# Row maxima carried as a row of the queries, biases folded into weights, and the exponentials' low half split by query half

## The reference, cut to what matters

```python
# layer 0: non-local attention per image, 64 embedding channels, no biases
f = softmax(theta.T @ phi / sqrt(64));  x = x + proj_w @ (f applied to x)
# layer 1: on tokens t (4, 1024, 128), z = layernorm(t)
keys = z @ Wk + bk; queries = z @ Wq + bq; values = z @ Wv + bv
t = t + softmax(queries @ keys.T / sqrt(128)) @ values
# layer 2: top 2 of 8 experts, z = layernorm(t)
gate = z @ Wg + bg; w = softmax(top 2 of gate)
t = t + sum over the two experts e: w_e * (gelu(z @ W1[e] + b1[e]) @ W2[e] + b2[e])
```

## Time and profile before

| | us |
|---|---|
| median of 3 runs | 565.32 (560.21 to 565.96) |
| span of the profiled execution | 603.2 |
| steps -2 and -1, to the first maximum of unit 1 | 0 to 41.4 |
| unit 0's step | 41.4 to 69.3 |
| units 1, 2, 3 | 69.3 to 103.5 to 137.0 to 172.7 |
| units 4, 5, 6 | 172.7 to 212.9 to 248.2 to about 278 |
| unit 7's step | 278 to about 318 |
| unit 7's outputs, routing, first tiles | 318 to 437 |
| experts | 437 to 575 |
| mixing, transposing, storing | 575 to 603.2 |

### The profile page before, as it was taken

The page is one execution under the profiler, slowest core; times in us unless marked ns, Lnnn a source line. Parts: engine busy times, 40 slices in busy tenths (PEclk is TensorE's granted clock), DMA queues, the critical chain, the costliest instruction groups (busy, mean ns, idle before and its releaser), DMA issues.

```text
span 603.2 us, 15423 instructions
## 1 busy us (share of the span) xinstructions
PE 431.2 (71%) x4139; PEld 313.6 (52%) x4140; DVE 431.8 (72%) x1303; ACT 300.6 (50%) x689; POOL 307.6 (51%) x352
## 2 busy tenths in 40 slices
PE   5668898999999899995952051610588898989626
PEld 3333565766666567663741041400476687878512
DVE  4897898988889788888684131781277788878737
ACT  4567766668866556663541000130265566656402
POOL 2012264555466654553787737027047677767720
PEclk9899999999999899998885565855699999999965
DMA  6100400000000130000011101004312222222166
GB/s 205 29 2 0 140 1 0 3 0 3 0 1 0 30 112 0 1 0 2 10 53 54 53 28 53 1 22 114 78 40 74 71 74 83 74 76 84 45 198 238
DMA packets 33493, 30.94 MB, mean 51 GB/s; under 512 B 8327, under 2 KB 27437, under 8 KB 33453
## 3 DMA queue, kind: packets, MB, share of 16 engines
q1 hardware_dynamic: 28844, 20.92, 12.2%
q0 software_dynamic: 4608, 9.51, 4.7%
HBM read 16.69 MB, written 13.73 MB: 50 GB/s over the span
## 4 chain that ended last, share of the span: by engine, by line
PE 25%; DVE 22%; issue 21%; POOL 8%; another core or an unknown queue 8%; ACT 7%; DVEq 3%; SPq 2%; DMA 2%; ACTq 1%; POOLq 0%
PE SC L529 8%; PE PV L529 7%; PE MX L529 6%; POOL ybuf L517 5%; PE PR L529 3%; DVE mx L1179 3%; ACT E L987 2%; DVE DG L1183 2%; ACT EH L911 1%; DVE TOK L1475 1%; DVE stats L1218 1%; DVE TOK L1480 1%; DVE QK L1137 1%; DVE TOK L1214 1%
## 5 line engine op out<-in xcount | busy, mean ns | idle before, releaser
L529 PE MATMUL PV<-VH,EH 128*128 128x129 f16 x512 | 98.2, 230 | 9.2 <-DVE TOK L1214 7.5
L529 PE MATMUL PV<-VL,EH 128*128 128x128 f16 x512 | 97.8, 226 | 3.6 <-issue 3.6
L529 PE MATMUL PV<-VH,EL 128*128 128x129 f16 x512 | 98.1, 228 | 2.2 <-issue 2.2
L474 POOL TENSOR_TENSOR EL<-E,EH 128x1024 f32 (+1 forms) x32 | 68.1, 2128 | 59.6 <-ACT EH L911 59.3
L517 POOL DMA_INDIRECT ybuf<-QK,yid x80 | 88.4, 1105 | 18.2 <-issue 12.8
L910 ACT ACTIVATE E<-SC 128x512 f32<-128x512 f32 x128 | 77.1, 602 | 37.5 <-PE SC L529 37.5
L529 PE MATMUL SC<-QK 128*128 128x512 f16 x320 | 91.0, 383 | 6.3 <-ACT EH L911 5.9
L438 POOL DMA_INDIRECT zbuf<-ZZ,posi x64 | 63.5, 993 | 51.9 <-DVE posi L1104 33.6
L1179 DVE TENSOR_REDUCE mx<-MX 128x1 f32<-128x1024 f32 x64 | 77.9, 1217 | 1.5 <-PE MX L529 1.1
L911 ACT ACTIVATE EH<-SC 128x512 f32 (+1 forms) x128 | 77.8, 608 | 0.0
L529 PE MATMUL MX<-EL,EH 128*128 x640 | 59.4, 246 | 2.7 <-issue 2.7
(11 more groups left out here) (195 smaller groups left out, 963.5 us busy)
## 6 DMA issues: line engine op xcount, KB each, us to landing
EH<-zbuf SPq DMA_DIRECT2D x40, 130.0 KB
X<-in_x_dram SPq DMA_DIRECT2D x4, 512.0 KB, 5.6
zbuf<-zer SPq DMA_DIRECT2D x16, 128.0 KB, 2.8
X<-in_L_ffn_W_dram SPq DMA_DIRECT2D x1, 2048.0 KB, 9.7
EL<-ybuf SPq DMA_DIRECT2D x4, 512.0 KB, 5.6
EH<-ybuf SPq DMA_DIRECT2D x4, 512.0 KB, 8.9
out_dram<-X SPq DMA_DIRECT2D x8, 256.0 KB, 3.0
ybuf<-QK,yid POOLq DMA_INDIRECT x80
```

Source lines behind the costliest of these rows:

```text
L474: nc.gpsimd.tensor_tensor(EL[:, u % 2, ds(i * 2 + 1, 1), :], E32[:, 1:2, :], EH[:, u % 2, ds(i * 2 + 1, 1), :], ALU.subtract).then_inc(e32 ...
L529: return nc.tensor.matmul(o, w, r, start=start, stop=stop)
```

## The change

- **Maxima as a row.** The reduction writes bf16. PE multiplies the column by minus the identity over a constant c (`row`: two products of one output row, 128 columns each, into MX[0:1]), ACT copies the row into channel 0 of the queries' low half, and the keys have the constant c in channel 0: so the scores' own matmuls subtract the maximum, and the diagonals and their matmuls go. In layer 0 the keys' halves are laid out so that a group of scores is two matmuls (was three), in layer 1 three (was four). A row of pair i is made in pair i+1 (PE behind the second group of scores, ACT behind the second exponentials), the last one in the first pair of the next step.
- **Constant channel 0.** POOL presets channel 0 of the normalised rows to 128. Since a layer norm sums to zero over the channels, the weights' row 0 can be subtracted from the others and the bias put in its place (`augment` on DVE in step -1, `expert_rows` on DVE ahead of unit 3's step). The bias matmuls, the gate's bias and the Gelu's bias go; Gelu becomes one instruction of 1024 columns.
- **Merged weights.** Layer 1's scores use Wq·Wkᵀ (`gram`): queries are projected with it, and the keys are the transposed rows themselves; the keys' projection of layer 1 goes.
- **Order.** Scores, exponentials and E32 go by query half: (p, h) = (0,0), (1,0), (0,1), (1,1). POOL makes EL of the first query half and does so first in its pair; DVE makes the second, now behind its second maximum.

GpSimd's presets stand ahead of its other constants, and PE's first instruction waits for all five:

```diff
+            nc.gpsimd.memset(QK[0:CE, :, 1, :], 0.0).then_inc(preset, 1)
+            nc.gpsimd.memset(QK[0:CE, :, 3, :], 0.0).then_inc(preset, 1)
+            pool.wait_ge(preset, 2)
+            nc.gpsimd.memset(QK[0:1, :, 3, :], TOP).then_inc(preset, 1)
+            nc.gpsimd.memset(ZZ[:, :, 0:1], CST).then_inc(preset, 1)
+            nc.gpsimd.memset(ZZ[:, :, P:P + 1], 0.0).then_inc(preset, 1)
```

GpSimd's pair:

```diff
-                    pool.wait_ge(sc_free, i * 4 + (2 * T * u + 6))
-                    nc.gpsimd.tensor_tensor(EL[:, u % 2, ds(i * 2 + 1, 1), :], E32[:, 1:2, :],
-                                            EH[:, u % 2, ds(i * 2 + 1, 1), :], ALU.subtract).then_inc(e32_free[1], 1)
+                    pool.wait_ge(sc_free, i * 4 + (2 * T * u + 4))
+                    c = slice(0, HALF)
+                    nc.gpsimd.tensor_tensor(EL[:, u % 2, ds(i * 2, 2), c], E32h[0], EH[:, u % 2, ds(i * 2, 2), c],
+                                            ALU.subtract).then_inc(e32_free[0], 1)
...
                 def pair(i, before):
+                    if u is not None:
+                        e_low(i)
                     if before is not None:
                         normalise(*before)
                         split(*before)
-                    if u is not None:
-                        e_low(i)
```

TensorE:

```diff
+                def row(unit, need):
+                    pe.wait_ge(mx_free, need)
+                    for p in range(2):
+                        last = mm(MX[0:1, p * P:(p + 1) * P], mxb[:, p:p + 1], negI[:, layer(unit), :], True, True)
+                    last.then_inc(mx_full, 1)
...
-                    pe.wait_ge(diag_ready, T * u + T // 2 * (h + 1))
-                    mm(o_, onesb[:], DG[:, u % 2, 4 * h:4 * h + 4, :], False, True).then_inc(sc_full, 1)
...
                     if u is not None:
-                        scores(i, 0, 1)
+                        scores(i, 1, 0)
+                    if first and u is not None:
+                        row(u, mx_base(s) + 1)
+                    if not first and m is not None:
+                        row(m, i * 3 + n_mx)
...
-                    if v is not None and v < UNITS:
+                    if v is not None and v < B:
                         projected("keys", i)
```

ScalarE:

```diff
+                def row(unit, c, need):
+                    act.wait_ge(mx_full, need)
+                    cp(QL[0:1, unit % 3, c], MX[0:1, 0:2 * P]).then_inc(mx_free, 1)
...
-                for c in range(HC):
-                    k = slice(c * TR, (c + 1) * TR)
-                    last = nc.scalar.activation(h32[:, b % 2, k], WIDE[b % 2][:, k], ACT.Gelu,
-                                                bias=b1T[:, ds(e * HC + c, 1)], scale=1 / WS)
-                last.then_inc(h_ready, 1)
+                nc.scalar.activation(h32[:, b % 2, :], WIDE[b % 2], ACT.Gelu, scale=1 / WS).then_inc(h_ready, 1)
```

VectorE (`augment`, `expert_rows`, the reduction):

```diff
+                nc.vector.scalar_tensor_tensor(out=W32[:, 2:5, :], in0=W0b[:], scalar=nvec[:, 0:1],
+                                               in1=W32[:, 2:5, :], op0=ALU.mult, op1=ALU.add)
...
+                nc.vector.scalar_tensor_tensor(out=Xw[:, c], in0=W10b[k // 2][:, k % 2 * S:(k % 2 + 1) * S],
+                                               scalar=nvec[:, 0:1], in1=Xw[:, c], op0=ALU.mult, op1=ALU.add) \
...
+                if s == 3:
+                    dve.wait_ge(w1_in, 16 * (2 + E))
+                    for k in range(PAIRS):
+                        expert_rows(k)
...
-                    nc.vector.reduce_max(mx[:, p:p + 1], MX[:], AX.X).then_inc(mx_free, 1)
+                    nc.vector.reduce_max(mxb[:, p:p + 1], MX[:], AX.X).then_inc(mx_free, 1)
```

More of the change, by code:

```diff
@@ L41 @@
 VW = P + 1
+CST = 128.0
+TOP = 2.0 ** 15
 E = 8
@@ L272, in build @@
                 {"values": (0, 0), "queries": (1, 0), "keys": (0, 1)},
-                {"rows": (0, 0), "values": (1, 0), "queries": (0, 1), "keys": (1, 1)},
+                {"rows": (0, 0), "values": (1, 0), "queries": (0, 1)},
                 {"rows": (0, 0), "logits": (1, 0)}]
@@ L925, in pair @@
                         high_x()
-                    if v is not None and v >= B:
+                    late = first and s == UNITS - 1
+                    if v is not None and v >= B and not late:
                         transposed(i)
                     if u is not None:
-                        exponentials(i, 0, 1)
+                        exponentials(i, 1, 0)
+                    if first and u is not None:
+                        row(u, slice(S - 2 * P, S), mx_base(s) + 1)
+                    if late:
+                        transposed(i)
+                    if not first and m is not None:
+                        row(m, ds(i * 256 - 256, 256), i * 3 + n_mx)
                     if first and v is not None and v < B:
@@ L1126, in _ @@
                 u, a, m, v = roles(s)
-                n_mx = mx_base(s) + (1 if v is not None and v < B else 0)
+                n_mx = mx_pairs(s)
                 if v is not None and v < B:
@@ L1311, in pair @@
                         statistics(i, 0)
+                        sums(i, 1)
                         counted(i, 0)
-                    if on_m:
-                        diagonals(i, 0)
+                    if on_v and v < UNITS:
+                        queries(i)
                     elif on_a:
```

300 lines of the change are left out of this document (164 added, 136 removed).

## The result

The changed kernel took 617.11 us (616.5 to 617.53, 4 runs) against 562.77 for the kernel before (558.85 to 565.96): ratio 1.097 [1.091, 1.102]. Forecast were 588, range 545 to 603: the side was right, but the rise is 54 us where 23 were forecast, and the time lies outside the range.

The account below looks back on a forecast made before the run. TensorE looked like the bound, with VectorE's work close beside it. 13.5 + 5.6 + 5.0 + 4.6 - 2 - 2 = +24.7, less 2 for overlap, about +23: 588 us for the median of 565.3, range 545 to 603.

Parts of the forecast that it names:

- the term for SP's queue: Ten W1 loads issued for one, row broadcasts some 60 us ahead, nothing waiting behind them in SP's queue: 0.
- the steps -1 to 1: First attention steps: pairs of step -1 +3.6 less 0.6, step 0 +2.0, step 1 +1.1.
- The pairs, +13.5: Attention pairs of units 0 to 6, four per step, mostly lengthened by new waits, unit 4 shortened: +13.5 us in all.
- the exclusion: GpSimd's low half (2.13 us) and certain VectorE instructions block each other, so VectorE's mean copy waits until R+3.3 in every pair.
- expert_rows, +4.6: Four VectorE operations of 1024 columns ahead of unit 3's step, 1.21 each, TensorE's values behind: +4.6 (0 to 6).
- The front, +5.6: TensorE's first instruction waits for GpSimd's presets, 10.8 instead of 4.30; first product from 9.33 to about 14.9: +5.6.
- nothing either way: ScalarE gains a row copy per pair (0.28) and loses or splits a key copy: no net cost.
- Step -1 and the borders: Step -1: `augment` +2.0, pairs +3.6 less 0.6, +5.0 together; 2 taken off the whole for overlap at step borders.
- Experts and unit 7's step, -4: One Gelu for four in the experts, -2; GpSimd's low half moved into its idle gap in unit 7's step, -2.
- Rival 1: The exclusion costs nothing, the mean copy slipping ahead of GpSimd's low half; pairs 7.7 to 7.9, 558 us; chance 0.27.
- rival 2: The engines' work decides, waits fall into slack; pairs 7.0 to 7.2 us, 537 us; chance 0.14.
- rival 3: Only the front costs; pairs as long as now, +15 less 4 left, 576 us; chance 0.14.

Follow-up runs that it names:

- e2: e1 with GpSimd's old order restored, normalise and split ahead of its low half: 659.7 us, kernel before beside it 607.8; stretch from first to last maximum 277.0.
- e6: e1 with VectorE's mean copy and variance addition each made by a sum over one element: 656.3 us, kernel before beside it 604.3; stretch 275.6.
- e1: Changed kernel with W1 loaded whole on 128 partitions and b1 laid over row 0 afterwards: 659.3 us, kernel before beside it 607.8; stretch 284.1.
- e3: Kernel before with its W1 load cut into partition 0, then partitions 1 to 127: 622.6 us against 607.8, 1.032 [1.020, 1.043].
- e14: Kernel before with its W1 load cut into partitions 0 to 126, then partition 127: 584.2 us against 564.8, one run.
- e9: e5 with the expert rows spread in eight instructions over steps 2 and 3, ScalarE's wait moved to its W1 scaling: 584.3 us, 1.037 [1.033, 1.041].
- e15: e10 with Wq, Wk, Wv and Wg loaded whole and biases laid over row 0: 581.2 us against 564.8, 1.027 [1.022, 1.033].
- e5: e2 with ScalarE's row copy ahead of tile 1's exponentials and VectorE's keys ahead of its low half at early step borders: 657.0 us against 604.3.
- e0: The changed kernel unedited, run again: 618.0 us against 564.2 for the kernel before, 1.098 [1.093, 1.103].
- e10: e9 with fills on VectorE and TensorE waiting for presets and constants only ahead of step -1: 582.8 us against 564.2, 1.026 [1.022, 1.030].
- e11: Kernel before with GpSimd's subtraction for W1's low half spread over steps 4 and 5: 559.7 us against 564.2, 0.992 [0.990, 0.995].

## Where the prediction failed, and where it held

The step that failed is the term for SP's queue, put at 0: it was worth some 16 us. Next come the steps -1 to 1, forecast 6.1 us longer and 17.7 longer in the trace. Point by point, the forecast against the traces:

- **The pairs, +13.5: the sum right, by two errors.** Steps 0 to 6 without the one long pair are 14.6 longer, but steps 2 to 6 only 3.8 (10.4 forecast) and steps 0 and 1 10.8 (3.1). Single pairs took 9.3 to 9.6 in step 2 (9.1 forecast), 9.6 to 9.7 in step 5 (9.3), 9.0 in step 1 (8.7), 9.0 to 9.3 in step 4 (9.3), 8.7 to 9.0 in step 3 (9.3), 8.2 to 8.5 in step 6 (8.9); and step 4's last pair fell from 11.64 to 9.15, which I had not looked at. The mechanism is shown: e2 and e6 take the exclusion away in two ways and get 7.1 and 8.5 us back. Two of its details were off: it strikes the mean copy in steps 1, 2, 4 and 5 (up to 2.13 us) and the square in steps 3 and 6 (up to 1.78), in all 14 of 32 copies and 22 of 32 squares over 0.3 us (4 and 1 before), not the copy in every pair; and with it gone the pairs return to the length before, not below.
- **SP's queue, "nothing waits in SP's queue behind them: 0": the step that failed.** The load of 127 partitions ran on one DMA engine and SP stood 74.66 us with the copies of row 0 behind it. I counted ten issues and did not price the one whose form had changed. Worth 15.7 us in the trace, 16.2 in e1; the form alone, in the kernel before, cost 19.2 (e3) and 18.0 (e14).
- **expert_rows, +4.6: the size right (4.9), its place not.** ScalarE's wait for the rows stands ahead of its exponentials of step 3; with that the rows cost 7.9 (the pair is 16.8 in e1, 8.9 in the kernel before) or 8.2 (8.6 in e9). I had put what is queued behind VectorE's instructions, not what is queued behind ScalarE's wait for them.
- **The front, +5.6: right to 0.2** (fills 2.65 against 2.6, first instruction 11.22 against 10.8, first product 15.06 against 14.9). To the first maximum I had 2.0 more, it was 4.0 more: 1.4 between the first product and the last key copy, where the keys' copy in two parts (0.77 instead of 0.38, in 4 pairs) was left at "nothing either way", and 2.5 from the low half of x to the maximum, where `augment` stands. e15 gets 6.1 of the 9.7 back.
- **Step -1 and the borders: too small.** Without the 2.0, step -1 was forecast +3.0 and is +6.9, step 0 +2.0 and is +5.8, step 1 +1.1 and is +5.0. The last pairs of these steps are 2.3 to 3.5 longer each, where I took 2 off "for what overlaps at the step borders". No clock was in the forecast, and part of this is the clock. Two pairs of step -1 (6.15, 4.9 forecast) ran at a granted clock of 0.50, the lower level of 1.2 GHz; the third took 5.32 at 0.82. Ahead of them TensorE had stood 3.63 us for the augmented weights (the two rows below). A pair of step 0 took 7.07 at 0.83, and 6.76 at 1.00 in e5 and e9 with their other edits; in the earlier trace rows it is 6.43 at 1.00. So some 1.7 us of step -1 and 1 us of step 0 are the clock, an estimate from these pairs; the border pairs, at 0.69 to 0.85, are not separated.

```profile
27.95 0.47 PE L586 MATMUL PV<-ident,W 128*128 128x128 f32 x1 [3.63 <-DVE W L1114]
...
41.80:47.10 5.30, 3.23 (x21) 1.93 (x20) 3.73 (x5) 1.90 (x5) 0.00 (x0) 0.82 0.00 0
```

- **Experts and unit 7's step, -4:** the Gelus, first to last, take 118.4 to 120.8 us in the changed kernel, e0, e9, e10 and e15 against 123.0 to 126.0 in e11 to e14, -2 to -8 for -2; unit 7's gain was not seen apart. The whole second half is 285 against 284.5 to 290.

Rival 1 (exclusion free) and rival 2 (the work decides) are refuted by the stretched copies and by pairs of 9.0 and more. Of rival 3, only the front, the pairs of steps 1, 2 and 5 refute "as long as now"; those of step 3, but for the first, did come out so (8.7 to 9.0 for 8.8 to 8.9).

Put together from the trace: first maximum 9.7, step -1 6.9, pairs 14.6, VectorE's wait 15.7, rows and ScalarE's wait 7.8, which is 54.7; on 562.8 that is 617.5, less 0 to 5 in the second half, against 617.1 measured.

## What to carry to other kernels

Price each DMA whose shape changes even when its data are wanted much later: look at the DMA share of its window (0.07 is one engine) and at the issue behind it. Take the full 128 partitions and overwrite a row afterwards rather than leave one out. Where two engines exclude each other, ask which instruction comes next after the one you free; and for every wait, list what stands behind it on the waiting engine.
